# Gated cross-attention with a routed FFN: the negative maxima's DMA moves to ScalarE, and TensorE's K product moves to the head of each step

## What is computed

```
x = x + tanh(g_xattn) * xattn(layernorm(x), ctx)     # 16 heads of 16, softmax over the 375 context rows
x = x + tanh(g_ffn) * moe(layernorm(x))              # 8 experts, the 2 best per row, SiLU gate, 256 -> 512 -> 256
q = x @ Wq;  k = ctx @ Wk;  v = ctx @ Wv
attn = softmax(q k^T / 4);  out = (attn v) @ Wo
```

## Time and profile before

| | |
|---|---|
| median of 3 runs | 632.15 us (629.47, 632.15, 634.42) |
| the profiled execution | 635.14 us, its span 633.4 us |
| TensorE matmuls busy | 501.3 us, 79% |
| VectorE, ScalarE, GpSimd busy | 429.8, 334.8, 290.6 us |
| mean granted TensorE clock | 0.903 |

### The profile page before, as it was taken

How to read it: one execution, slowest core, us unless ns; L and a number is a source line. 1 busy time by engine, 2 the same in 40 slices (tenths; PEclk the granted TensorE clock), 3 DMA queues, 4 the chain that set the end, 5 groups by cost and what they waited for, 6 DMA issues and landing times. The chain is left out here.

```text
span 633.4 us, 15041 instructions
## 1 busy us (share of the span) xinstructions
PE 501.3 (79%) x4738; PEld 451.4 (71%) x4739; DVE 429.8 (68%) x906; ACT 334.8 (53%) x623; POOL 290.6 (46%) x251
## 2 busy tenths in 40 slices
PE   3467598889889999999988862169888999999940
PEld 2356487778878888888877652159787999999940
DVE  1754376878868999899988857667776555555520
ACT  2332164557645776676764657057666545554520
POOL 9300263445524556545454731251545666555340
PEclk9998587988979999999998985569899999999985
DMA  8347835785648865775844319872634443333234
GB/s 189 125 105 203 177 107 120 188 210 148 175 98 214 220 165 149 203 203 130 210 97 124 96 40 342 244 248 76 169 93 67 70 68 58 57 59 59 34 40 126
DMA packets 75373, 87.19 MB, mean 138 GB/s; under 512 B 26904, under 2 KB 63600, under 8 KB 75136
## 3 DMA queue, kind: packets, MB, share of 16 engines
q1 hardware_dynamic: 67264, 75.54, 45.1%
q0 software_dynamic: 8064, 11.06, 10.7%
HBM read 60.99 MB, written 27.30 MB: 139 GB/s over the span
## 5 line engine op out<-in xcount | busy, mean ns | idle before, releaser
L347 POOL TENSOR_TENSOR PL<-PT 125x448 f16<-125x448 f32 x96 | 100.3, 1047 | 150.8 <-ACT PT L463 150.6
L727 DVE TENSOR_REDUCE mx<-bank 112x1 f32<-112x375 f32 x256 | 130.6, 542 | 46.7 <-PE bank L561 44.9
L463 ACT ACTIVATE PT<-bank 125x448 f32<-125x448 f32 x192 | 103.8, 544 | 93.1 <-PE bank L576 92.3
L1316 POOL DMA_INDIRECT acc_scr<-ys,slot_row x42 | 68.8, 1637 | 85.8 <-ACT ys L1356 77.0
L561 PE MATMUL bank<-KS,QS 97*112 97x376 f32 x256 | 91.6, 382 | 13.7 <-DVE mx L727 11.2
L576 PE MATMUL bank<-QS,KS 98*125 98x256 f32 x384 | 85.5, 308 | 14.3 <-DMA QS<-nm 13.4
L576 PEld LDWEIGHTS bank<-QS,KS 98*125 98x125 f32 x384 | 68.4, 198 | 16.3 <-DMA QS<-nm 9.9
L1390 PE MATMUL bank<-xH,GH 128*128 128x256 f16 x336 | 66.1, 279 | 6.4 <-ACT sg L1341 5.8
L1390 PE MATMUL bank<-xL,GH 128*128 128x256 f16 x336 | 65.8, 279 | 0.0
L1390 PE MATMUL bank<-xH,GL 128*128 128x256 f16 x336 | 65.4, 277 | 0.0
L561 PEld LDWEIGHTS bank<-KS,QS 97*112 97x112 f32 x256 | 46.7, 187 | 25.1 <-DVE mx L727 21.7
(11 more groups left out here) (213 smaller groups left out, 1097.1 us busy)
## 6 DMA issues: line engine op xcount, KB each, us to landing
KS<-k_scr SPq DMA_DIRECT2D x48, 376.0 KB
k_scr<-kH SPq DMA_DIRECT2D x16, 376.0 KB, 2.5
k_scr<-kL SPq DMA_DIRECT2D x16, 376.0 KB, 3.1
QS<-q_scr SPq DMA_DIRECT2D x96, 56.0 KB, 4.7
ctx_sb<-in_ctx SPq DMA_DIRECT2D x16, 281.2 KB
wsq<-in_L_ffn_gate_w SPq DMA_DIRECT2D x8, 512.0 KB, 4.2
wsq<-in_L_ffn_up_w SPq DMA_DIRECT2D x8, 512.0 KB, 5.4
w_raw<-in_L_ffn_gate_w SPq DMA_DIRECT2D x8, 512.0 KB, 5.4
```

What stands on the lines that cost most here:

```text
L347: pool.tensor_tensor(PL[:, 2 * k:2 * k + 2, :, 0:N], PT[:, 2 * k:2 * k + 2, :, 0:N], PH[:, 2 * k:2 * k + 2, :, 0:N], ALU.subtract).then_in ...
L463: act.activation(PT[:, 2 * k:2 * k + 2, :, 0:N].rearrange("p a e i -> p (a e) i"), psST[k % 2][0:JP].rearrange("p (a i) -> p a i", i=NI)[: ...
L727: dve.tensor_reduce(mx[:, hd:hd + 1], psS[hd % 2][0:N, 0:M], AX.X, ALU.max).then_inc(v_max, 1)
L1316: pool.indirect_dma_start(acc_scr, bass.IndirectOffsetOnAxis(ap=slot[:, TH * t + k:TH * t + k + 1].bitcast(U32), axis=0), ys[:, u, k, :], ...
```

## The change

The DMA of nm and its wait leave SyncE's step and stand in ScalarE's, in slot MT + 2 = 10, ahead of oTH and of that slot's exponential. `KP` becomes (0, 1), and on TensorE the half K product of a slot stands ahead of L576. As kH and kL follow `KP`, they too come one slot earlier.

```diff
-        KP = (1, 2)
+        KP = (0, 1)
...
-                    if live(i, c, 1):
-                        b, h, u = at(i, c - 1)
-                        sp.wait_ge(v_nm, b + 1)
-                        sp.dma_start(f32(QS[u][RM:RM + 1, :, :, 0:N]).rearrange("o q e i -> o (q e) i"),
-                                     f32(nm[:])).then_inc(d_m[u], 16)
...
+                        if k == MT + 2 and live(i, c, 1):
+                            b, h, u = at(i, c - 1)
+                            act.wait_ge(v_nm, b + 1)
+                            act.dma_start(f32(QS[u][RM:RM + 1, :, :, 0:N]).rearrange("o q e i -> o (q e) i"),
+                                          f32(nm[:])).then_inc(d_m[u], 16)
...
+                        if s in KP and live(i, c, 0):
+                            project_k(i, c, KP.index(s))
                         if s < SB and live(i, c, 2):
                             scores_T(i, c, s)
-                        if s in KP and live(i, c, 0):
-                            project_k(i, c, KP.index(s))
```

## The result

The changed kernel takes 679.65 us, median of 4 runs (670.02 to 683.75), against 630.81 us for the kernel before (4 runs, 624.55 to 634.42). The ratio is 1.069, interval 1.061 to 1.077: 7% slower. Executions more than 1.5% above a kernel's fastest are left out of the ratios of this document, but not out of its medians. The profiled execution has 670.02 us and a span of 668.3; it is the fastest of the four, so the trace shows 35 us of the loss.

What follows compares the result with a forecast made beforehand. Bound by TensorE and VectorE handing banks to each other, with VectorE's chain of maxima in each quiet step. Terms +10.5, -4.0 and -4.1 gave +2.4 us on the median of 632.15: 634.5 us, range 622 to 648.

Steps and rivals of the forecast that it cites:

- The prediction's own signs of being wrong: Late periods near 18 to 18.7 us, a 0.50 clock in late steps, L576 still behind nm, or nm landing over 4.7 us.
- first issue to second: First attention step: TensorE starts at 73.7 rather than 77.85, since the half K product needs only cTL; -4.1 us.
- next six steps: Early steps: waits for nm and their lowered clock go, so 20.16 us a step becomes 19.5; -4.0 us.
- last seven steps: Later steps, with hardly any wait for nm to save: each costs 1.5 us more, 18.00 becoming 19.5; +10.5 us.
- The late start and the longer chain: VectorE's maxima in each step: chain starts 0.7 us later and takes 0.6 more; with ScalarE's 0.2, 1.5 us a step.
- Four waits: TensorE ahead of the scores of heads 4 to 7 waits about 0.45, 0.5, 0.45 and 0.95 us, lacking the half product.
- The clock: Slower rival, chance 0.21: bunched waits lower TensorE's clock in every second step, 2.4 us a fall, 14.6 in all, giving 649 us.
- SyncE no longer waits for nm ... that is worth nothing by itself: SyncE's issues in the steps: squares' weights and context come some 3 us earlier, nobody waits for them, so no gain.
- a landing of 4.4 us or less: nm's transfer: the median landing of 4.4 us is covered, as its first use comes 4.7 us after the issue.
- nm doesn't stand behind the reload of KS on a queue of its own: nm's DMA on ScalarE's queue: the small transfer would pass the KS reload issued before it; no separate size given.
- The first wait: TensorE's 6.01 us wait for nm at 77.85: the half K product starts at 73.7 instead, worth -4.1 us.
- ScalarE's issue: nm's DMA issue behind an exponential on ScalarE late in each step: delays the step's end by 0.2 us, bounds 0 and 0.6.

Runs made afterwards that it cites:

- k_fill: k_only with ten small matmuls that nobody reads, spread over the waits ahead of the scores of heads 4 to 7: 641.0 us, ratio 1.018 to the kernel before.
- k_only: The kernel before with only KP = (0, 1) and TensorE's new order, nm's DMA still on SyncE: 670.4 us, ratio 1.058.
- dma_only: The kernel before with only nm's DMA moved from SyncE to ScalarE, TensorE's order and KP kept: 677.3 us, ratio 1.071.
- dma_sp: dma_only with SyncE still waiting for nm at its old place, a 64-byte copy there, before its later loads: 632.1 us, ratio 1.005 to the kernel before.
- kp_only: The kernel before with only KP = (0, 1), kH and kL moving with it, TensorE's order within a slot kept: 674.9 us, ratio 1.072.

## Why the prediction was wrong

It said 634.5 us, within 1%, range to 648; measured 679.7. The forecast's sum had no term for a lower clock in the steps, and it took nm's landing as covered. These two steps failed. The prediction's own signs of being wrong came with them: the 0.50 level in late steps, and landings over 4.7 us.

By stages, with (1 - clock) x length for what the clock takes:

| | forecast | measured | of it the clock |
|---|---|---|---|
| first issue to second | -4.1 | +4.3 | +5.5 |
| next six steps | -4.0 | +7.7 | +5.8 |
| last seven steps | +10.5 | +22.7 | +13.4 |

*The late start and the longer chain*, 1.5 us a step with ScalarE's part, were about right. Four waits of 0.45, 0.5, 0.45 and 0.95 were forecast, 0.44, 0.53, 0.29 and 0.85 came. Without the clock the last seven steps cost 9.3 us more, 1.3 each. In k_fill the same seven steps, between these two issues,

```profile
215.45 0.56 SPq L299 DMA_DIRECT2D QS<-nm  x1
...
349.96 0.56 SPq L299 DMA_DIRECT2D QS<-nm  x1
```

take 19.2 us each, against 18.00 before, small matmuls included: 1.2 for what I had at 1.3.

*The clock* is the term that failed the forecast. I had it as a rival at 0.21, with the argument that each piece is under 1 us and that a wait of 0.41 was followed by no fall. Single waits were the wrong thing to compare: 0.44, 0.53, 0.29 and 0.85 close together were followed by the 0.50 level in eight of 13 steps, as one wait of 1.83 was the earlier trace rows. The rival's count was good, six falls forecast and seven periods more than before in the trace. Its price was too low: (82 - 37) / 2 = 22 us over seven are 3.2 us each, not 2.4. At that price the rival would have said 654. The first stage, which holds nm's 8.0 us, spends nearly all its time at the lower level (0.55). k_only alone lost about 40 and gets 29 back by the clock.

*"SyncE no longer waits for nm ... that is worth nothing by itself"* is the second step that failed. I looked for who waits for the loads, and not for what the loads make wait. The wait on SyncE kept the context and, in most steps, wsq behind nm, and taking it away alone cost 47 us (dma_only against dma_sp). I gave nm a landing of 4.4 us or less and a due time 4.7 us after the issue; in dma_only it was 6.1 by the median, in the changed kernel 5.8 to 6.3 in four late steps and 3.9 by the median.

*nm doesn't stand behind the reload of KS on a queue of its own* found no support: the first landing, issued right behind the reload, took 6.6 us on SyncE's queue in before, and on ScalarE's 5.4 in dma_only, 7.0 in dma_sp and 8.0 in the changed kernel, where the context and the first queries are issued just ahead of it too. With nothing in flight it took 1.8 on SyncE's queue (k_only's issue at 232.06, with a DMA share of 0.00 from 231 to 233). The Trainium skill's rule that I set against the change ("DMA: Bandwidth & Descriptors", section "Issuing engines are not separate DMA queues") holds here, by dma_only's 6.1 against dma_sp's 4.2. From the turns between queues of the same page's section "Queues, rings and completion order" I had nm pass what stood in another queue; its 7 KB did not pass quickly here.

*The first wait*, worth 4.1 us: TensorE did begin the half product before nm came, but cTL and nm were both later, and the second issue is at 101.04, not before 93.56. From the first issue to the second it is 26.6 us, where before has 22.4. That gain never came.

*ScalarE's issue*, 0.2 us: right in this step. oTH starts 0.66 behind the exponential (229.65 to 230.31), where it was 0.44, and the last PV group waits 0.21 for the PL.

## What to carry to other kernels

Where TensorE's work is moved off a stretch in which it waits for another engine, add up all its waits in that stretch, not the longest alone. If the stretch becomes sparse, give what follows a price at the lower clock in the sum itself; here it was more than the waits. Then look at the clock of every step, as the same waits need not be followed by a fall each time. Before a wait is taken off a queue of DMA issues, list what stands behind it: the wait may be what keeps large loads behind a small transfer that somebody needs soon. When two edits are made at once, time each alone, since the losses need not add.

## What was not expected of the hardware

- Small matmuls that nobody reads, 140 in all, made the k_only kernel faster: 670.4 to 641.0 us in the waits, and 686.5 when put where TensorE hardly waits. In the kernel before, whose clock is up already, they cost about 6 us.
- A transfer of 7 KB took 1.8 us when nothing was in flight (k_only) and 6.1 by the median on a queue of its own, behind loads that were issued up to 3 us earlier on SyncE's (dma_only). 0.3 MB of them were enough: 7.7 us at 253.23.
- What stays open is why the same four waits were followed by a fall in eight steps and not in five, what besides kL's place makes kp_only's loss, and by what nm is held up behind so small a load.
